# Sixteen-head attentions: two PSUM banks in turn for the query and key projections, one bank for the turned probabilities, and queries and keys turned one item later

## The reference, cut to what matters

```python
def _L1_xattn_ref(emb, context, Wq, Wk, Wv, Wu, bu, qn_w, qn_b, kn_w, kn_b):
    q = (emb @ Wq.T).reshape(B, SQ, N_HEADS, KQ_DIM).transpose(0, 2, 1, 3)
    k = (context @ Wk.T).reshape(B, SK, N_HEADS, KQ_DIM).transpose(0, 2, 1, 3)
    v = (context @ Wv.T).reshape(B, SK, N_HEADS, KQ_DIM).transpose(0, 2, 1, 3)
    q = _layernorm(q, qn_w, qn_b)
    k = _layernorm(k, kn_w, kn_b)
    attn = jnp.einsum('bhqd,bhkd->bhqk', q, k) * scale
    attn = jax.nn.softmax(attn, axis=-1)
    out = jnp.einsum('bhqk,bhkd->bhqd', attn, v)
    return out @ Wu.T + bu

def _L2_xattn_ref(q, context, mask, Wq, Wkv, Wout, b_out):
    qp = q @ Wq
    k, v = jnp.split(context @ Wkv, 2, -1)
    attn = jnp.einsum('bhid,bhjd->bhij', qh, kh) * scale
    attn = jnp.where(mask[:, None, None, :], -jnp.inf, attn)
    attn = jax.nn.softmax(attn, axis=-1)
    out = jnp.einsum('bhij,bhjd->bhid', attn, vh)
    return out @ Wout + b_out
```

## Time and profile before

| | us |
|---|---|
| median of three runs | 1621.97 |
| lowest, highest | 1621.96, 1628.43 |
| the profiled execution's own time | 1623.44 |
| span of the profiled execution | 1621.7 |
| TensorE busy in the span | 1397.8 (86%) |
| VectorE busy | 839.1 (52%) |
| ScalarE busy | 728.3 (45%) |
| mean granted TensorE clock | 0.92 of full |

### The profile page before, as it was taken

The page is one execution under the profiler, slowest core; times in us unless marked ns, Lnnn a source line. Parts: engine busy times, 40 slices in busy tenths (PEclk is TensorE's granted clock), DMA queues, the critical chain, the costliest instruction groups (busy, mean ns, idle before and its releaser), DMA issues. The chain is left out here.

```text
span 1621.7 us, 27487 instructions
## 1 busy us (share of the span) xinstructions
PE 1397.8 (86%) x9061; PEld 1085.9 (67%) x9061; DVE 839.1 (52%) x2258; ACT 728.3 (45%) x1657; POOL 146.7 (9%) x256
## 2 busy tenths in 40 slices
PE   6765689999998789959999997995499996999995
PEld 5631367777777457749999995994377773667664
DVE  4548466666664445445454553345777772122224
ACT  4341466666664311225555553342255551433433
POOL 1010000000000000000000002004233430000000
PEclk9878699999999799969999997996599995999998
DMA  8000000000000000000000001202000000000000
GB/s 323 1 1 0 1 1 2 1 1 1 1 1 1 1 1 1 1 0 1 1 2 1 1 1 43 75 2 104 0 1 1 0 1 0 1 1 1 0 1 26
DMA packets 6429, 24.55 MB, mean 15 GB/s; under 512 B 797, under 2 KB 1311, under 8 KB 5418
## 3 DMA queue, kind: packets, MB, share of 16 engines
q1 hardware_dynamic: 6314, 23.03, 4.1%
HBM read 21.98 MB, written 1.05 MB: 14 GB/s over the span
## 5 line engine op out<-in xcount | busy, mean ns | idle before, releaser
L1304 DVE SCALAR_TENSOR_TENSOR XN<-bank,gate,XN 128x128 f32<-128x128 f32 x256 | 89.9, 351 | 224.7 <-PE bank L1268 222.2
L1284 ACT ACTIVATE e_hidden<-bank,small 128x512 f32<-128x512 f32 x152 | 104.4, 687 | 214.5 <-PE bank L1256 214.5
L765 PE MATMUL bank<-a_va,a_pT 128*128 128x65 f32 x1024 | 130.3, 270 | 0.7 <-ACT a_pT L931 0.6
L1009 DVE TENSOR_REDUCE a_mx<-bank 128x4 f32<-128x512 f32 x128 | 87.8, 686 | 80.2 <-PE bank L805 80.1
L1268 PEld LDWEIGHTS bank<-attention_weights,e_hidden 128*128 128x128 f32 x1024 | 119.2, 192 | 14.8 <-issue 14.8
L765 PEld LDWEIGHTS bank<-a_va,a_pT 128*128 128x128 f32 x1024 | 125.2, 193 | 2.4 <-ACT a_pT L931 1.1
L1256 PE MATMUL bank<-XNT,attention_weights 128*128 128x512 f32 x256 | 121.2, 606 | 1.3 <-PEq L541 1.3
L1268 PE MATMUL bank<-attention_weights,e_hidden 128*128 128x128 f32 x1024 | 119.3, 275 | 0.0
L830 PE MATMUL bank<-attention_weights,a_cv 128*128 128x256 f32 x256 | 84.4, 411 | 15.5 <-issue 15.5
L931 ACT ACTIVATE a_pT<-bank 128x512 f32<-128x512 f32 x128 | 76.1, 595 | 41.9 <-PE bank L839 39.2
L1017 DVE TENSOR_TENSOR a_shifted<-bank,a_mx 128x512 f32<-128x512 f32 x128 | 88.3, 690 | 3.4
(11 more groups left out here) (351 smaller groups left out, 2718.2 us busy)
## 6 DMA issues: line engine op xcount, KB each, us to landing
attention_weights<-in_a SPq DMA_DIRECT2D x2, 2048.0 KB, 11.6
mod_ring<-in_mod_weights SPq DMA_DIRECT2D x4, 576.0 KB
ctx_both<-in_ctx SPq DMA_DIRECT2D x1, 2048.0 KB, 10.1
attention_weights<-in_up SPq DMA_DIRECT2D x1, 2048.0 KB, 7.6
attention_weights<-in_down SPq DMA_DIRECT2D x1, 2048.0 KB, 13.2
down<-in_down SPq DMA_DIRECT2D x1, 1536.0 KB, 18.5
down<-in_mod_weights SPq DMA_DIRECT2D x2, 576.0 KB
X<-in_x SPq DMA_DIRECT2D x4, 256.0 KB, 3.5
```

Source lines behind the costliest of these rows:

```text
L765: last = pe.matmul(value_bank[:, j * (W + 1):(j + 1) * (W + 1)], pT[:, i.slot(2), j * 128:(j + 1) * 128], va[:, p, g // 2 * 8 + 2 * j + g ...
L1009: dve.tensor_reduce(mx[:, i.slot(2), :], score_bank[i.slot(2)][:, :].rearrange("p (h s) -> p h s", h=4), AX.X, ALU.max).then_inc(maxed, 1)
L1284: act.activation(hidden[0:rows, p, f, :], up_bank_of(i, f)[0:rows, :], function, bias=up_bias(g, f)).then_inc(hidden_ready, 1)
L1304: dve.scalar_tensor_tensor(out=total, in0=down_bank[j][:, e * D:(e + 1) * D], scalar=gate_column(k, 4 * q + j, g * per_group + e), in1=tot ...
```

## The change

Three edits in `stage_head_attention`, for both attentions unless said otherwise.

1. `project_bank` becomes two banks, used in turn by item number. `project_qk` of item m waits until the bank of item m-2 is free (before: item m-1).
2. `turn_bank` becomes one bank. `turn_p` of item m waits until `keep_p` of item m-1 is done (before: item m-2).
3. In attention 1 alone, `turn_qk` and `keep_qk` move one iteration later, and with them everything behind them (scores to turn_x). The pipeline is 13 iterations deep instead of 12. The lags of attention 2 stay.

```diff
     if qk_norm is not None:
-        lag = {"square": 1, "turn_qk": 1, "keep_qk": 2, "scores": 5, "project_v": 5, "subtract": 5, "exponentials": 6,
-               "turn_p": 7, "keep_p": 7, "values": 9, "turn_o": 11, "out": 11, "normalise": 12, "turn_x": 12}
+        lag = {"square": 1, "turn_qk": 2, "keep_qk": 3, "scores": 6, "project_v": 6, "subtract": 6, "exponentials": 7,
+               "turn_p": 8, "keep_p": 8, "values": 10, "turn_o": 12, "out": 12, "normalise": 13, "turn_x": 13}
     else:
         lag = {"keep_qk": 1, "scores": 4, "project_v": 4, "subtract": 4, "exponentials": 5,
                "turn_p": 6, "keep_p": 7, "values": 8, "turn_o": 10, "out": 10, "normalise": 11, "turn_x": 11}
...
-        score_bank, turn_bank = [k.ps[0], k.ps[1]], [k.ps[2], k.ps[3]]
-        value_bank, project_bank, qkt_bank, out_bank = k.ps[4], k.ps[5], k.ps[6], k.ps[7]
+        score_bank, project_bank, turn_bank = [k.ps[0], k.ps[1]], [k.ps[2], k.ps[3]], k.ps[5]
+        value_bank, qkt_bank, out_bank = k.ps[4], k.ps[6], k.ps[7]
...
             def turn_p(i):
                 m, p = i.number, i.slot(2)
                 await_count(pe, exped, m + 1)
-                if i.older_than(2):
-                    await_count(pe, p_kept, m - 1)
+                if i.older_than(1):
+                    await_count(pe, p_kept, m)
                 for j in range(4):
-                    last = pe.transpose(turn_bank[p][:, j * 128:(j + 1) * 128],
+                    last = pe.transpose(turn_bank[:, j * 128:(j + 1) * 128],
                                         probs[:, p, j * 128:(j + 1) * 128], k.ident)
                 last.then_inc(p_turned, 1)
 
             def project_qk(i):
...
-                if i.older_than(1):
-                    await_count(pe, qk_normed if qk_norm is not None else qk_kept, m)
+                if i.older_than(2):
+                    await_count(pe, qk_normed if qk_norm is not None else qk_kept, m - 1)
+                bank = project_bank[i.slot(2)]
```

More of the change, by code:

```diff
@@ L850, in project_qk @@
                 if qk_norm is not None:
-                    last = pe.matmul(project_bank[:, :], source[:, p, :],
+                    last = pe.matmul(bank[:, :], source[:, p, :],
                                      weight[:, half * 512:(half + 1) * 512], start=True, stop=True)
@@ L855, in project_qk @@
                         at_pair = (half * 4 + j) * 128
-                        last = pe.matmul(project_bank[:, j * 128:(j + 1) * 128],
+                        last = pe.matmul(bank[:, j * 128:(j + 1) * 128],
                                          weight[:, at_pair:at_pair + 128], source[:, p, :],
@@ L890, in square @@
                     await_count(act, ssq_ready, i.number)
-                act.activation(sq[:, :], project_bank[:, :], ACT.Square).then_inc(squared, 1)
+                act.activation(sq[:, :], project_bank[i.slot(2)][:, :], ACT.Square).then_inc(squared, 1)
             def keep_o(i):
@@ L908, in keep_qk @@
                 await_count(act, qk_turned if qk_norm is not None else qk_projected, m + 1)
-                bank = qkt_bank if qk_norm is not None else project_bank
+                bank = qkt_bank if qk_norm is not None else project_bank[i.slot(2)]
                 if g == 0 and i.older_than(8):
@@ L930, in keep_p @@
                     await_count(act, weighted, m - 1)
-                act.activation(pT[:, p, :], turn_bank[p][:, :], ACT.Copy).then_inc(p_kept, 1)
+                act.activation(pT[:, p, :], turn_bank[:, :], ACT.Copy).then_inc(p_kept, 1)
             def keep_v(i):
@@ L1002, in normalise_qk @@
                 dve.tensor_tensor(qn[:, p, :].rearrange("p (h w) -> p h w", w=W),
-                                  project_bank[:, :].rearrange("p (h w) -> p h w", w=W),
+                                  project_bank[p][:, :].rearrange("p (h w) -> p h w", w=W),
                                   ssq[:, p, :].unsqueeze(2).to_broadcast([128, 8, W]),
```

## The result

| | before | after |
|---|---|---|
| median, us | 1621.97 | 1643.11 |
| lowest to highest of four runs, us | 1617.24 to 1628.43 | 1642.19 to 1645.05 |
| span of the profiled execution | 1621.7 | 1640.4 |
| mean granted TensorE clock | 0.920 | 0.927 |

The changed kernel is slower: the ratio of the times is 1.0126, with a 95% interval of 1.0107 to 1.0145, or +21 us.

What follows compares the result with a forecast made beforehand. TensorE was taken to wait about 7% of attention 1's steady stretch and to bound attention 2, busy 217.00 of 217.00 us. Terms -14 - 12 - 1.5 + 55 - 2.5 = +25 on the median gave 1647 us, range 1634 to 1664.

Steps and rivals of the forecast that it cites:

- The loss in attention 2: Attention 2, steady and drain: turn_p waits for ScalarE's copy of the same iteration, 44 x 1.2 us plus 3: +55 us.
- the last four waits: Attention 2, drain: four more waits of about 0.7 us, since values waited for the same copy anyway: 3 us.
- the clock falls in attention 2: Rival, attention 2: the new waits make TensorE's clock dip about once a batch, +22 us, 1669 us; chance 6%.
- The head and the drain of attention 2 without the wait: Attention 2: only its head was forecast to gain, through two projection banks, -2.5 us, between -3.5 and 0.
- the three idle times of 0.78 us: Attention 2, head: three projections wait 0.78 us each for keep_qk; with two banks they don't.
- Attention 1, steady: Attention 1, some 13.5 batches: the wait ahead of project_qk goes, 1.04 us a batch: -14 us, bounds 9 and 17.
- The three waits of 0.25, 0.56 and 0.23 us: Attention 1, steady: project_qk waits for normalise_qk of the item before in three iterations, 1.04 us a batch.
- the bound: Attention 1, steady: a gain of 17 us if each restart also costs some 0.08 us.
- Attention 1, head and drain: Attention 1: first values earlier by -12 us (-7 to -14); drain with one projection less beside it, -1.5 us (-3 to 0).
- an iteration costs what TensorE needs at its lower clock: Attention 1, head: from the third projection an iteration takes 2.9 us; four end at 183.7, 6.3 us earlier.
- The wait that stays: Attention 1, iterations without scores: project_v still waits for keep_qk, 3.02 us after the projection; no gain taken.
- attention 1 gains twice as much: Rival, attention 1: project_v's wait goes too, 18 us, and a faster head: no change, 1622 to 1630 us; chance 6%.

Runs made afterwards that it cites:

- The kernel with the earlier copy: Against the changed kernel, attention 2's copy of the turned probabilities (keep_p) has lag 6 instead of 7, the same as turn_p: 1578.6 us.

## Why the prediction was right, and where its terms were off

**The loss in attention 2.** Its mechanism was right in each step: idle ahead of the turned probabilities, ended by ScalarE's copy, in three of four iterations, with TensorE busy 85% (forecast 82 to 86%) and a batch of 20.47 us (forecast 20.3). One wait delays `turn_p` by 1.70 - 0.49 = 1.21 us, and a batch grows by 20.47 - 16.73 = 3.74 us, 1.25 per wait against the 1.2 that I took.

The kernel with the earlier copy has everything of the change but this wait, so the two attentions 2 give its whole price: 341.9 - 276.9 = 65.0 us, where the sum had 55. Twelve steady batches hold 45 of them. The head (first projection to first L113) is 44.6 instead of 37.05 us, 7.5 more, which is six waits. The last three intervals between updates are 19.57, 19.0 and 13.1 us instead of 15.91, 12.08 and 11.0: +12.7 us. The sum had 3 us for the last four waits, since values waited for the same copy there anyway, and the step that failed is this one. By the count (47, less 36 in the twelve batches and six in the head) five waits fall here, 6 us at 1.25. The other 6 lie where the granted clock was lower than in the kernel with the earlier copy; no run separates that part from the waits. The view by stretches over the last 23 us of the stage, and the timeline:

```profile
994.60:1017.60 23.00, 19.79 (x92) 17.53 (x90) 3.63 (x13) 4.78 (x12) 0.00 (x0) 0.57 0.00 1
```

```profile
997.01 1.06 PE L839 MATMUL bank<-consts,a_probs 128*128 128x128 f32 x4
...
1000.75 3.72 PE L818 MATMUL bank<-attention_weights,a_oT 128*128 128x128 f32 x16
```

The granted clock is 0.57 there, and single operations run at the lower of the two levels: turned probabilities in 1.06 instead of 0.60 us, the output in 3.72 instead of 2.05 us. In the kernel with the earlier copy the last 23 us have 0.95, in the kernel before 0.79:

```profile
930.00:953.00 23.00, 19.35 (x147) 16.67 (x146) 8.87 (x27) 8.86 (x22) 0.00 (x0) 0.95 0.00 1
975.70:998.70 23.00, 18.88 (x113) 15.67 (x112) 6.64 (x21) 7.35 (x18) 0.00 (x0) 0.79 0.00 1
```

So a fall of the clock belongs to this drain in the kernel before as well, where TensorE was never idle in the steady stretch, and it is deeper in the changed one. The rival "the clock falls in attention 2" is borne out in the last 30 us alone and not in the steady stretch, where it had put its 22 us. In the steady stretch the clock was 1.00 in all three kernels with this wait, with three idle times of 1.05 us a batch and TensorE busy 84 to 85%. The Trainium skill (TensorE: Matmul & The Clock Gate, section A second HAM failure mode: psum-queue depth-cycling) tells of another kernel, in which TensorE is briefly idle between groups of matmuls as PSUM banks cycle and the clock swings; this stretch doesn't show it. What decides in the drain stays open. The change in attention 2 alone has the same instructions and the same waits there, yet its stage was 337.8 us, 4.1 shorter, all of it in the drain, with less of the fall:

```profile
1030.00:1053.00 23.00, 18.23 (x109) 15.77 (x110) 6.09 (x19) 6.67 (x16) 0.00 (x0) 0.82 0.00 1
```

**The head and the drain of attention 2 without the wait.** Forecast -2.5, measured 276.9 - 287.1 = -10.2 us: -7.1 in the head (37.05 against 44.2) and -3.1 in the drain. The head is the second projection bank's: the pair of kernels that differ in it alone has 5.9 us there. The drain isn't assigned: the earlier copy also takes away two waits of 0.3 us of the values for the same copy, and no run has the second projection bank with two banks for turned probabilities. The step that failed was to count only the three idle times of 0.78 us. It left out a fourth of 0.34 us, and the lower clock at which the head ran for its first 14 us:

```profile
711.60:725.90 14.30, 11.97 (x55) 10.45 (x56) 1.48 (x3) 3.28 (x7) 1.31 (x6) 0.50 0.00 0
720.00:730.00 10.00, 9.60 (x65) 8.27 (x66) 2.81 (x5) 3.51 (x7) 0.53 (x2) 0.70 0.00 0
```

And in the changed kernel, from the same point of the stage (first projection 711.58 before, 675.72 after):

```profile
670.00:680.00 10.00, 4.29 (x21) 4.31 (x21) 3.38 (x4) 2.97 (x4) 1.53 (x7) 0.66 0.00 0
680.00:690.00 10.00, 9.30 (x86) 8.13 (x85) 5.34 (x8) 6.05 (x14) 0.82 (x3) 1.00 0.00 0
```

Between 4 and 14 us after its first projection TensorE does 86 matmuls at a clock of 1.00; before, between 8 and 18 us after it, 65 at 0.70. It had no idle time between the projections, and the clock rose earlier. That the one brought the other is inferred from this pair and from the pair without the earlier copy.

**Attention 1, steady.** Forecast -14; (20.68 - 19.44) x 13.5 = -17 us measured. The three waits of 0.25, 0.56 and 0.23 us are gone, 1.04 us a batch; the remaining 0.2 is the restart of some 0.08 us behind each, which I had left for the bound. A projection took 1.10 us behind a wait (L851 in the earlier trace rows) and 1.02 without one. The second bank, with the lags as they were, took 32.0 us off the stage, where TensorE had been waiting for the reader of its only projection bank. The Trainium skill's sentence that PSUM double-buffering "gave no further gain" (TensorE: Matmul & The Clock Gate, section HAM oscillation) is about another matmul kernel; carried over, it would have made this term zero, and the measurement goes against that.

**Attention 1, head and drain.** The head was -15.2 us (43.2 to 28.0), forecast -12. Further profiles of the same code gave 46.4 and 41.5 us for the old head and 27.6 and 28.0 for the new, so it is 13.5 us at the least. The forecast had the first scores 15.5 us after the first projection (183.7 - 168.23), and they came after 12.6. The step that failed was "an iteration costs what TensorE needs at its lower clock": the projection at 175.64 already took 1.10 us, 9 us after the first, and the scores 1.16. In the kernel before the projection 3.9 us after the first one still took 2.04 us, as did one 23 us into the stage where the lags alone were changed. What is left of the -35.0 us is the drain, -2.8 for a forecast of -1.5, too little apart to say more.

**The wait that stays.** `project_v` behind `keep_qk` stayed at 2.94 to 3.02 us after the projection, as forecast, and none of it was lost or won. The reason that I gave for it was half of it: I named the square in front of `keep_qk`, but the exponentials between the two could be moved away, which was worth 6.5 us. The rival "attention 1 gains twice as much" had asked for that wait to go, and took it for impossible by ScalarE's order; the order was free to change.

**The sum.** The terms were 55 us for the wait (measured 65), -2.5 for the second projection bank in attention 2 (-10.2), and -27.5 for attention 1 (-35.0). Three errors of 10, 8 and 8 us, of both signs, left 4 us by the medians: +25 forecast, +21 measured. That the total came so near is in part luck: the mechanisms were right, but each of the three sizes was further off than their sum.

## What to carry to other kernels

A buffer can be taken away when the copy that frees it is issued an iteration ahead of the step that reuses it; where the copy stands in the same iteration behind another step of the chain, a single buffer makes the engines wait for each other once per iteration. Look at the lag of the freeing step before counting buffers: here one number, a lag of 6 instead of 7, was the difference between +21 and -44 us. And once an engine's wait is gone, read its list of waits again, since the next one (`keep_qk`, then `keep_o`) was worth another 13.6 us for moving two steps in ScalarE's order.

## What the runs showed of the hardware

At the head of both stages TensorE's granted clock was higher where it stood idle less. With idle times of 2.1 to 2.8 us ahead of the projections of attention 1 the clock was 0.56 over the first 12.7 us and 0.53 over the first 21.8 us (168.2 to 190.0); with two banks it was 0.73 over the first 12.7 (166.7 to 179.4). In the head of attention 2 four idle times, 2.7 us together, went with the second bank, and the head was 7.1 us shorter. So idle time in a head can cost more than its own length. In the steady stretch idle times of 1.05 us, three in 20.5 us, left the clock at 1.00.

Where TensorE waited for ScalarE's copy, 0.14 us passed from the end of the copy to the start of the first matmul (831.98 to 832.12). The group behind a wait took longer: 0.63 instead of 0.60 us for the turned probabilities, and 1.10 instead of 1.02 us for the projection.
